# Folding the second feed-forward weight in the QKV stage: two products of split operands for one fp32 product, and another order of the preparation

## The reference

```
mod = (silu(c) @ wmod).reshape(2, 6, 1, 512)          # sa, ca, ga, sb, cb, gb
h = layernorm(x) * (1 + ca) + sa
x = x + ga * attention(h, Wqkv, Wproj, bproj)
h = layernorm(x) * (1 + cb) + sb
hidden = fwht(silu(h @ W1.T) * (h @ W3.T))             # 2048 wide, scaled by 1/sqrt(2048)
x = x + gb * (hidden @ W2.T)
```

## Time and profile before

| | us |
|---|---|
| median of 3 runs | 3094.98 |
| lowest and highest of them | 3094.19, 3102.08 |
| the profiled execution's own time | 3104.26 |
| its span | 3102.4 |
| busy: TensorE matmuls | 3071.7 |
| busy: VectorE | 1883.1 |
| busy: ScalarE | 1514.0 |
| busy: GpSimd | 1420.4 |

### The profile page before, as it was taken

One profiled execution on the slowest core, in us unless ns is written; L12 is line 12 of the kernel. 1 busy time (PEld: TensorE's weight loads), 2 busy tenths in 40 slices (PEclk: granted clock), 3 DMA queues, 4 the chain that ended last, 5 costly groups with the idle time before them and its releaser, 6 DMA issues. The chain is left out here.

```text
span 3102.4 us, 41542 instructions
## 1 busy us (share of the span) xinstructions
PE 3071.7 (99%) x15568; PEld 2102.2 (68%) x15568; DVE 1883.1 (61%) x3182; ACT 1514.0 (49%) x2853; POOL 1420.4 (46%) x491
## 2 busy tenths in 40 slices
PE   7999999999999999999999999999999999999999
PEld 5888755555555555555555554778888888888887
DVE  5445988888888888888888873643232323323222
ACT  4333366666666666666666666543222222222221
POOL 2223378888888888888888884000000000000000
PEclk8999999999999999999999999999999999999999
DMA  7666578888888888888888876752211112111111
GB/s 252 197 203 184 157 157 178 183 181 179 177 182 182 181 181 176 181 183 181 181 176 181 182 158 172 258 196 77 87 45 62 58 48 72 44 62 59 47 61 35
DMA packets 149400, 446.40 MB, mean 144 GB/s; under 512 B 26961, under 2 KB 44625, under 8 KB 114002
## 3 DMA queue, kind: packets, MB, share of 16 engines
q0 software_dynamic: 28592, 204.48, 31.9%
q1 hardware_dynamic: 119554, 239.25, 25.9%
q10 hardware_dynamic: 1056, 0.00, 0.0%
HBM read 166.85 MB, written 80.21 MB: 80 GB/s over the span
## 5 line engine op out<-in xcount | busy, mean ns | idle before, releaser
L1280 DVE TENSOR_REDUCE mxp<-pmax 128x1 f32<-128x512 f32 x1968 | 1202.3, 680 | 246.7 <-PE pmax L1055 246.7
L1226 ACT ACTIVATE prob<-pexp 128x512 f32<-128x512 f32 x2023 | 1019.9, 627 | 407.9 <-PE pexp L1104 404.9
L1055 PE MATMUL pmax<-k,q 96*128 96x512 f32 x1968 | 813.3, 413 | 4.9 <-DVE mxp L1280 3.9
L1104 PE MATMUL pexp<-q,k 98*128 98x512 f32 x2023 | 805.3, 400 | 0.6 <-ACT prob L1226 0.6
L53 PE MATMUL pproj<-h2f,w 128*128 128x512 f32 x3072 | 717.4, 389 | 0.0
L53 PEld LDWEIGHTS pproj<-h2f,w 128*128 128x128 f32 x3072 | 576.5, 188 | 119.5
L1359 POOL TENSOR_TENSOR gsum<-gsum,prob 128x2048 f32<-128x2048 f32 x127 | 583.5, 4595 | 38.4 <-ACT prob L1226 29.2
L1055 PEld LDWEIGHTS pmax<-k,q 96*128 96x128 f32 x1968 | 374.2, 190 | 287.1 <-DVE mxp L1280 173.2
L1975 POOL TENSOR_TENSOR x2f<-sil,x2f 128x512 f32<-128x512 f32 x1 | 1.3, 1282 | 1192.6 <-DVE sil L1965 1192.6
L1115 PE MATMUL pctx<-prob,v 128*32 128x512 f32 x4096 | 497.5, 602 | 0.0
L1359 POOL TENSOR_TENSOR gsum<-prob 128x2048 f32<-128x2048 f32 x96 | 457.8, 4769 | 36.3 <-ACT prob L1226 36.2
(11 more groups left out here) (147 smaller groups left out, 1754.3 us busy)
## 6 DMA issues: line engine op xcount, KB each, us to landing
gsum<-prob POOLq DMA_DIRECT2D x187, 1024.0 KB, 7.4
w<-w_scratch SPq DMA_DIRECT2D x128, 256.0 KB, 2.6
q<-q_scratch SPq DMA_DIRECT2D x96, 256.0 KB, 4.4
k<-k_scratch SPq DMA_DIRECT2D x96, 256.0 KB, 6.1
q_scratch<-obq SPq DMA_DIRECT2D x32, 512.0 KB, 5.2
k_scratch<-obq SPq DMA_DIRECT2D x32, 512.0 KB, 3.7
xin<-in_L_attn_query_dram SPq DMA_DIRECT2D x8, 1024.0 KB, 8.0
v_scratch<-vst SPq DMA_DIRECT2D x8, 1024.0 KB, 5.0
```

The source lines that it names most:

```text
L1055: pe.matmul(pmax[:, bank, :], qst[slot][0:KR, qt * P:(qt + 1) * P], kst[slot][0:KR, kc * TOK:(kc + 1) * TOK], start=True, stop=True).then_ ...
L1104: pe.matmul(score_bank(g, n), kst[slot_of(g)][:, kt * P:(kt + 1) * P], qst[slot_of(g)][:, j * TOK:(j + 1) * TOK], start=True, stop=True).t ...
L1226: act.activation(prob_tile(g, kt)[:, j * TOK:(j + 1) * TOK], score_bank(g, n), ACT.Exp, scale=SCALE).then_inc(exp_done, 1)
L1280: dve.tensor_reduce(mxp[:, par, u // QJ, u % QJ:u % QJ + 1], pmax[:, bank, :], X, ALU.max).then_inc(mx_done, 1)
```

## The change

1. The sign product. The turned quarter is split: ScalarE rounds it to fp32r (`w2_high_half`, where `wt` lies), VectorE writes the difference (`w2_low_half`, where `wn` lies; new function `fold_low`, four subtractions, after result 9 of a fold tile). The signs are copied to fp32r once. TensorE does two fp32r products for each of the four fp32 products.
2. Because the low half lies in `wn`, the load of the next quarter waits for the products (`w2_mm`), not for the turn (`w2_turned`).
3. The preparation's order. ScalarE computes the SiLU of c and a square root of ones ahead of its first `high`, and takes the root of tile 0 after `high(2)`, not before it. VectorE starts the statistics after `low(0)` and does `low(1)` while the root is taken. TensorE does `modulate` ahead of `turn_tokens`, and `turn_mod` ahead of `turn_out(2)` and `turn_out(3)`; ScalarE's last two `out_high` go behind the modulation.

```diff
--- before.py
+++ after.py
@@ -76,6 +76,7 @@
         rest = keep["rest"] = sb("rest", [P, DC, (6 - NOW) * D])
         nat = sb("nat", [P, DC, QKV, D])
         ct = sb("ct", [P, DC, B])
+        root_one = sb("root_one", [P, 1])
         sc, one, mod = (keep[k] for k in ("sc", "one", "mod"))
         ps = ctx.enter_context(nc.psum_tensor("ps_prep", [P, DC, D], F32))
 
@@ -192,15 +193,15 @@
                     turn_rows(j)
                 turn_out(0)
                 turn_out(1)
+                pe.wait_ge(silu_done, 1)
+                for k in range(DC):
+                    modulate(k)
                 pe.wait_ge(row_hi, QKV * DC)
                 pe.wait_ge(row_lo, QKV * DC)
                 turn_tokens(pe, pt, xn, ident, keep["normed"], keep["turned"], 0)
-                pe.wait_ge(silu_done, 1)
-                for k in range(DC):
-                    modulate(k)
+                turn_mod()
                 turn_out(2)
                 turn_out(3)
-                turn_mod()
 
             @block.scalar
             def _(act):
@@ -218,13 +219,14 @@
                 with nc.allow_non_contiguous_dma("c is 1024 numbers"):
                     for b in range(B):
                         act.dma_start(ct[:, :, b], ins["c"][b].rearrange("(k p) -> p k", p=P)).then_inc(ct_in, 16)
-                high(0)
-                high(1)
                 act.wait_ge(ct_in, 16 * B)
                 act.wait_ge(set_up, 2)
                 act.activation(sc[:, :, 0:B], ct[:, :, :], ACT.Silu).then_inc(silu_done, 1)
+                act.activation(root_one[:, :], one[:, :], ACT.Sqrt)
+                high(0)
+                high(1)
+                high(2)
                 take_root(act, keep["chain"], keep["rooted"], 0, keep["dev"][:, :])
-                high(2)
                 high(3)
                 normal_tokens(act, xn, keep["xin"], keep["nmr"], keep["rstd"], keep["stats"], keep["x_in"],
                               keep["normed"], 0)
@@ -232,8 +234,6 @@
                 out_high(1)
                 act.wait_ge(mod_mm, DC)
                 act.activation(mod[0:NOW * HD, :], ps[0:NOW * HD, 0, :], ACT.Copy).then_inc(mod_read, 1)
-                out_high(2)
-                out_high(3)
                 act.wait_ge(mod_turned, 1)
                 for g, x in enumerate((SA, CA)):
                     src = by_chunk(ps[:, MOD_BANK, :])[:, :, g * HD:g * HD + B]
@@ -243,6 +243,8 @@
                         act.activation(dst, src, ACT.Identity, bias=one[:, 0:1]).then_inc(mod_taken, 1)
                     else:
                         act.activation(dst, src, ACT.Copy).then_inc(mod_taken, 1)
+                out_high(2)
+                out_high(3)
 
             @block.vector
             def _(dve):
@@ -260,10 +262,9 @@
                 dve.memset(sc[:, :, :], 0.0).then_inc(set_up, 1)
                 dve.memset(one[:, :], 1.0).then_inc(set_up, 1)
                 low(0)
-                low(1)
                 dve.wait_ge(keep["x_in"][0], 16)
                 norm_stats(dve, keep["chain"], keep["rooted"], 0, keep["xin"][0][:, :, :], keep["st"], keep["mv"],
-                           keep["dev"][:, :], keep["rstd"][:, 0, :], keep["nmr"][:, 0, :]).then_inc(keep["stats"], 1)
+                           keep["dev"][:, :], keep["rstd"][:, 0, :], keep["nmr"][:, 0, :], lambda: low(1)).then_inc(keep["stats"], 1)
                 low(2)
                 low(3)
                 for j in range(DC):
@@ -304,7 +305,7 @@
 LINKS = 4
 
 
-def norm_stats(dve, chain, rooted, t, x, st, mv, dev, rstd, nmr):
+def norm_stats(dve, chain, rooted, t, x, st, mv, dev, rstd, nmr, meanwhile=None):
 
     base = LINKS * t
     for k in range(TK):
@@ -317,6 +318,8 @@
     last.then_inc(chain, 1)
     dve.wait_ge(chain, base + 2)
     dve.tensor_scalar(dev, mv[:, :, 1], EPS, None, ALU.add).then_inc(chain, 1)
+    if meanwhile:
+        meanwhile()
     dve.wait_ge(rooted, t + 1)
     dve.reciprocal(rstd, dev).then_inc(chain, 1)
     dve.wait_ge(chain, base + 4)
@@ -391,8 +394,12 @@
         ht = sb("ht", [P, 2, 2, DC, TOK], F32R)
         vst = keep["vst"] = sb("vst", [P, 2, NH, TK, HD])
         ob = sb("obq", [P, OB, 2, TOK], F32R)
+        with ExitStack() as halves:
+            w2_low_half = halves.enter_context(nc.sbuf_tensor("w2_low_half", [P, HID], F32R))
+            w2_high_half = halves.enter_context(nc.sbuf_tensor("w2_high_half", [P, HID], F32R))
         wn = sb("w2n", [P, HID])
         wt = sb("w2t", [P, HID])
+        signs = sb("signs", [P, P], F32R)
         mark = sb("mark2", [P, 1])
         ps = ctx.enter_context(nc.psum_tensor("ps_qkv", [P, BANKS, TOK], F32))
 
@@ -400,7 +407,9 @@
         w2_fly = sem("a_w2_butterfly")
         w2_turned = sem("a_w2_turned")
         w2_taken = sem("a_w2_taken")
+        w2_lowered = sem("a_w2_lowered")
         w2_mm = sem("a_w2_mm")
+        signs_set = sem("a_signs_set")
         w2_scaled = sem("a_w2_scaled")
         w2_out = sem("a_w2_out")
         gains_out = sem("a_gains_out")
@@ -512,10 +521,13 @@
                 def fold_mult(t):
 
                     n = FOLD_AT.index(t)
-                    pe.wait_ge(keep["had_in"], 16)
+                    pe.wait_ge(signs_set, 1)
                     for i in range(DC):
                         pe.wait_ge(w2_taken, DC * n + i + 1)
-                        pe.matmul(pt[:, i, :], had[:, :], wt[:, i * D:(i + 1) * D], start=True, stop=True).then_inc(w2_mm, 1)
+                        pe.wait_ge(w2_lowered, DC * n + i + 1)
+                        pe.matmul(pt[:, i, :], signs[:, :], w2_high_half[:, i * D:(i + 1) * D], start=True, stop=False)
+                        pe.matmul(pt[:, i, :], signs[:, :], w2_low_half[:, i * D:(i + 1) * D], start=False,
+                                  stop=True).then_inc(w2_mm, 1)
 
                 def ring_item(i):
 
@@ -590,11 +602,14 @@
                 def fold_take(t):
 
                     n = FOLD_AT.index(t)
-                    if n:
+                    if n == 0:
+                        act.wait_ge(keep["had_in"], 16)
+                        act.activation(signs[:, :], had[:, :], ACT.Copy).then_inc(signs_set, 1)
+                    else:
                         act.wait_ge(w2_out, 16 * n)
                     for i in range(DC):
                         act.wait_ge(w2_turned, DC * n + i + 1)
-                        act.activation(wt[:, i * D:(i + 1) * D], pt[:, i, :], ACT.Copy).then_inc(w2_taken, 1)
+                        act.activation(w2_high_half[:, i * D:(i + 1) * D], pt[:, i, :], ACT.Copy).then_inc(w2_taken, 1)
 
                 def high_parts(t):
                     b = t // ST
@@ -731,10 +746,21 @@
                                 ring_item(i)
                         if t == 0 and j == REST_TURN:
                             gains()
+                        if j == FOLD_TURN and t in FOLD_AT:
+                            fold_low(t)
                         if j == MID + 1 and t + 1 < TILES:
                             low_parts(t + 1)
                     if t in FOLD_AT:
                         fold_scale(t)
+
+                def fold_low(t):
+
+                    n = FOLD_AT.index(t)
+                    dve.wait_ge(w2_turned, DC * (n + 1))
+                    for i in range(DC):
+                        dve.wait_ge(w2_taken, DC * n + i + 1)
+                        dve.tensor_tensor(w2_low_half[:, i * D:(i + 1) * D], pt[:, i, :],
+                                          w2_high_half[:, i * D:(i + 1) * D], ALU.subtract).then_inc(w2_lowered, 1)
 
                 def fold_scale(t):
 
@@ -765,7 +791,7 @@
 
                 for n in range(DC):
                     if n:
-                        pool.wait_ge(w2_turned, DC * n)
+                        pool.wait_ge(w2_mm, DC * n)
                     pool.dma_start(wn[:, :], ins["w2"][n * P:(n + 1) * P, :]).then_inc(w2_in, 16)
                     if n:
                         pool.wait_ge(w2_scaled, DC * n)
```

## The result

The changed kernel takes 3106.41 us, median of 7 executions (3102.94 to 3108.15), beside 7 of the kernel before on the same chip with a median of 3094.98 (3094.19 to 3102.08). The paired comparison gives a ratio of 1.0029, with a 95% interval of 1.002 to 1.0039: +9.0 us. The prediction was +7.1 us and 3102.1, in a range of 3088 to 3109.

What follows compares the result with a forecast made beforehand. TensorE, busy 3071.7 of 3102.4 us, was taken to bound the kernel. Products and waits together (+2.8), clock (+6.5) and preparation (-2.2) gave +7.1 us on the median 3095.0: 3102.1, range 3088 to 3109.

Steps and rivals of the forecast that it cites:

- What bounds the kernel: Whole kernel: TensorE is busy 3071.7 of 3102.4 us, so differences ahead of attention reach the end one for one.
- The sign products: QKV stage's W2 folds: fp32r pairs save 1.65 us a fold, 6.6 in four; the new subtractions cost nothing.
- The fourth rival: Sign products: split operands run like fp32, so no speedup, +6.6 us on any case; chance 0.02.
- The moved load: W2 folds: next quarter's load pushes the store of `wt` and first butterfly by 2.4 us, 1 in tile 0.
- What is late next: TensorE waits at result 11 of tiles 1 and 3 and tile 5's W2 turn: 2.3, 3.1 and 4.3 us.
- the walk: Tiles 1, 3, 5: stepping through alternating subtractions and butterflies; subtractions end at T + 29.9, 32.7, 35.5 and about 36.1.
- The clock: Behind each of the three TensorE waits, a stretch at 1.2 GHz costing 1.8, 2.1 and 2.6 us: +6.5.
- The preparation: Before the QKV stage: the new order starts the stage at 31.75 for 33.90, -2.2 us.
- The sum: Whole kernel: +2.8 + 6.5 - 2.2 = +7.1 us; 3102.1 on the median, 3111.4 on the profiled execution.
- (1) Fair sharing of the transfers: Fold's DMA: queues share packet by packet, store lands at about T + 11.5; -6.4 us, 3088.6; chance 0.17.
- (2) Waits without a cost of clock: QKV stage: the three waits come but no slow stretch follows; +0.6 us, 3095.6; chance 0.14.
- (3) Every wait with the clock stretch of the earlier trace: QKV stage: full-length 1.2 GHz stretch behind each wait, store pushed by 3.1 us; +12.8, 3107.8; chance 0.15.

Runs made afterwards that it cites:

- e7: Changed kernel with low half in the tokens' full-value buffer (early load), full values kept in PSUM, and token load behind the q stores; 0.9966 against the kernel before, 3084.73 us.
- e3: Changed kernel with the low half laid over the tokens' full values, so the next quarter's load is as early as before; 0.9995 against the kernel before, 3095.31 us.
- e5: Changed kernel with the tokens' full values kept in PSUM, so the low-part subtraction reads one SBUF source; 0.9983 against the kernel before, -5.3 us.
- e2: Kernel before with only the split sign products and their later load, the preparation as before; 1.0026 against the kernel before, 3106.71 us.
- e6: Changed kernel with the token load put behind the tile's four q stores, the W2 load still late; 0.9992 against the kernel before, -2.5 us.
- e1: Kernel before with only the preparation's new order; 0.9987 against the kernel before, median 3094.61 us.
- e8: Kernel before with the bias's low part set to zero, leaving out its one-row two-SBUF subtraction; 0.9996 against the kernel before, 3093.35 to 3096.68 us.

## Why the prediction was right or wrong

**What bounds the kernel.** Right: what the waits, the clock, the products and the preparation add up to reached the end of the stage within 2 us, and the end of the run within the 2.4 us just shown.

**The sign products.** Right. In e7, where nothing waits, the time from one fold's first product to the next over two tiles is 72.41 us twice (75.46, 147.87, 220.28), for 74.36 and 74.06 before: 1.65 to 1.95 us a fold, for a predicted 1.65. The fourth rival, that split operands run like fp32, is refuted by the pitch of 0.23 us. The new subtractions (229.28 to 231.76, ahead of the product at 234.53) cost nothing, as said.

**The moved load.** The mechanism was right: a transfer queued later, in another queue, comes after what was queued before. The delay of the first butterfly was predicted as 1, 2.4 and 2.4 us; it was 2.8, 4.5 and 2.6. Tile 4's was right; those of tiles 0 and 2 were taken too small. In tile 0 I let the token load fall partly behind the store; the two moved side by side. In tile 2 the delay is larger than the load's whole 3.1 us. The load was issued at 156.6 to 157.1, and until 162 only the other queue moved anything (DMA by queue, the changed kernel, 156 to 162 and 162 to 165.9; packets, MB, share of 16 engines):

```profile
q1 hardware_dynamic: 2413, 1.76, 110.6%
```
```profile
q0 software_dynamic: 153, 1.09, 70.5%
q1 hardware_dynamic: 179, 0.33, 22.2%
```

The load's wait is no delay of its own, as the store would have stood behind the same transfers. Then the store had the engines to itself, and what was left of it at 168.5 was slow (166 to 168, and 168.5 to 170.8):

```profile
q0 software_dynamic: 194, 0.79, 101.7%
q1 hardware_dynamic: 2, 0.00, 0.5%
```
```profile
q1 hardware_dynamic: 395, 0.77, 99.6%
q0 software_dynamic: 22, 0.05, 6.3%
```

The next tile's q stores, issued on SyncE's queue from 165.5 on, filled the engines, and the store's last 0.05 MB took until the butterfly at 170.76. In the kernel before the store was done before the q stores began (165.90 and 166.16). By these numbers the 1.4 us beyond the load's own 3.1 lie in the store's end; why the last packets take so long beside a later transfer, no run tells. The prediction's upper end, the load's packets' time at full rate, was thus no bound.

**What is late next.** All three waits were named with their places and their releasers, and all were sized too small: 3.8, 4.7 and 5.8 us for 2.3, 3.1 and 4.3. Two terms are behind that. One is the delay. In the walk the fourth subtraction was a short one; with butterflies later than it assumed, all four met one in tiles 1 and 3. The walk itself holds where the delay is small: between its own points (0.7 us at no delay and 2.3 at 1 us in tile 1; 1.0 and 3.1, and 1.5 and 4.3, at none and 2.4 us in tiles 3 and 5) e3's delays of 0.8, 1.7 and 0.7 us give an estimate of 2.0, 2.5 and 2.3, for 2.2, 2.2 and 2.3 measured. The other term is the butterflies' own length. In tile 5 the exclusion went the other way, the butterfly of 4.6 us, and lengthened the chain on which the turn waits: eight butterflies from 249.26 to 271.1, 21.8 us, where the walk had 20.4 (T + 14.5 to T + 34.9) and the kernel before 20.03. e5 shows that the exclusion is needed for two of the waits.

**The clock.** Right in kind: a stretch at 1.2 GHz stands behind each wait. It cost 8.5 us for a predicted 6.5. The half clock doesn't follow the length of the wait in any simple way: 4.1 us were followed by 6.9 (e2), 4.7 by 3.4 in one kernel and 6.8 in another, and of six waits of about 2.2 us in e3 and e6 three were followed by 3.4 us and three by nothing. A mean over such waits is all that could have been forecast.

**The preparation.** Sized too small: -3.5 (-3.1 in e1) for -2.2, though e1 has -2.2 left at the end of the stage. The changed kernel, to be laid beside the earlier trace rows, with the clock in `modulate`'s stretch:

```profile
17.52 2.79 PE L161 MATMUL ps_ht<-ident,nat 128*128 128x128 f32 x12 [2.48 <-DVE wv L255]
...
21.64 3.63 PE L180 MATMUL ps_prep<-wm,sc 128*32 128x512 f32 x16
...
25.20 1.97 PE L279 MATMUL ps_ht<-ident,xn 128*128 128x128 f32 x16
...
30.39 2.79 ACT L620 ACTIVATE ht<-ps_ht,shift,scale 128x512 fp32r<-128x512 f32 x4 [1.13 <-PEq L122]
```
```profile
21.20:24.60 3.40, 3.40 (x18) 1.11 (x18) 1.89 (x3) 3.40 (x6) 0.00 (x0) 0.99 1.05 416
```

The fourth group of transposes starts at 17.52 (predicted 17.9) behind the wait for `low(1)`, as said. The step that failed is the clock: I took half clock until 24, and the row shows 0.99 from 21.2 on, so that `modulate` took 3.63 us wholly at full clock and the first `ht` comes at 30.39, not 31.8.

**The sum.** Against the lower group of the kernel before, the terms are: -6.6 (predicted -6.6), waits +14.0 (+9.4), clock +8.5 (+6.5), preparation -3.5 (-2.2): +12.4 for +7.1. The ratio of the runs, +9.0, is nearer to the forecast than its terms are. That is luck: it comes about because the kernel before is slower in part of its executions by a collision that the changed kernel's profile doesn't have. I had read that collision in the earlier trace rows as the price of a wait only, and not asked whether it belonged to every execution. The forecast for the profiled execution, 3111.4, was 4.1 us above the 3107.3 measured: 5.0 too little for the stage, the 7 us of the earlier trace rows counted as staying, and 2 us from elsewhere that I haven't traced.

**The rivals.** (1) Fair sharing of the transfers is refuted by the butterflies at T + 14.7 to 16.5 and by the empty queue 0 until 162. The Trainium skill, "DMA: Bandwidth & Descriptors", section on queues, rings and completion order, has the engines go round the queues with work; the later-issued transfer of this case didn't get such a share. Only where two were issued at the same moment, in tile 0, did both queues move together (86 to 90 us). A rival that I hadn't named, that SyncE's queue always goes ahead of GpSimd's, is refuted by the rows of 166 to 168: the q stores were issued on SyncE's queue from 165.5 on, and the store on GpSimd's queue moved 0.79 MB before they moved anything; in the kernel before, q stores issued at 166.16 were moving by 167. (2) Waits without a cost of clock: refuted. (3) Every wait with the clock stretch of the earlier trace rows and a push of the whole load: +12.8 predicted. By the account of the stage this is the case that came true, two of three stretches being 6.8 us, and the push being 2.6 to 4.5; by the measured ratio it is the forecast. I gave it 0.15.

## What to carry to other kernels

A scratch buffer reused for a new operand moves the point at which its next load can be issued; count the megabytes that then stand ahead of the transfer somebody waits for, whatever queue they are in, and walk on to who is late. Here a saving of 6.6 us was turned into a loss by that one dependence, and lending the operand another idle buffer, keeping the subtraction's source in PSUM and issuing the token load later gave all of it back. Ask of each stall in the baseline's profile whether every execution has it.

## What the runs showed of the hardware that was not expected

- Transfers of two queues issued one behind the other were served in the order of issue: 2, 3 and 4 MB ahead and with the store gave a first butterfly 9 to 11, 12 to 13.6 and 14.5 to 16.6 us after the product, and an issued load moved nothing for 5 us. It holds in both directions between the two queues, except for the last packets of a transfer: 0.05 MB took 2.3 us beside 0.77 MB of later ones.
- A VectorE subtraction with two SBUF sources of a single row (1x512) took 5.83 us behind a GpSimd sum of 4.83 us, for 0.68 alone; the four subtractions of a tile took 10.62 us for 2.8. With one source in PSUM they took 0.68 each beside butterflies of 2.4 us (e5). It also went the other way, a butterfly taking 4.6 us while VectorE did four in a row.
- Such a collision, met in some executions and not in others of the same program, was worth some 7 us and made two groups of times (e8, and e1's 12 executions).
- Waits of TensorE of about 2.2 us were followed by 3.4 us at 1.2 GHz in three cases and by full clock in three others.
